# The second MLP product of the first phase in three bf16 terms, with new orders on four engines

## What is computed

```python
x = x + tanh(g_xattn[0]) * L0_xattn(layernorm(x), ctx, ctx, ...)
def L0_xattn(q, k, v, ...):
    log_ratio = log(prob(q)) - log(prob(k))            # prob: tanh, scaled and normalised
    sid = einsum('bnd,bmd->bnm', prob(q) - prob(k), log_ratio)
    attn = softmax(-sid / sqrt(D))
    f_diff = (v - attn @ v) @ W_diff.T + b_diff + q
    h = layernorm(f_diff, ln_g, ln_b)
    mlp = gelu(h @ W1.T + b1) @ W2.T + b2              # W1: 1024 x 256, W2: 256 x 1024
    return layernorm(mlp + f_diff, ln_g, ln_b)
```

## Time and profile before

| | us |
|---|---|
| median of three runs | 1754.54 |
| lowest and highest | 1752.0, 1756.51 |
| the profiled execution, its own time | 1753.54 |
| its span, first to last instruction | 1751.8 |

### The profile page before, as it was taken

How to read it: one execution, slowest core, us unless ns; L and a number is a source line. 1 busy time by engine, 2 the same in 40 slices (tenths; PEclk the granted TensorE clock), 3 DMA queues, 4 the chain that set the end, 5 groups by cost and what they waited for, 6 DMA issues and landing times.

```text
span 1751.8 us, 42950 instructions
## 1 busy us (share of the span) xinstructions
PE 1610.3 (92%) x14411; PEld 1255.7 (72%) x14411; DVE 1336.3 (76%) x3213; ACT 1055.9 (60%) x1894; POOL 1033.6 (59%) x1873
## 2 busy tenths in 40 slices
PE   5999999999999993577999999999999999999997
PEld 4888888888888882344677777767777776767666
DVE  5677777777777766768888888888888888887643
ACT  6666666666666553255656666665666666565654
POOL 5566676667666645324656575665656566564536
PEclk9999999999999996688999999999999999999999
DMA  7312211221122002342233232322223232222200
GB/s 210 101 61 74 76 60 60 75 75 60 60 79 71 7 1 71 96 123 79 82 83 88 79 93 75 90 85 82 81 83 90 72 90 85 83 84 84 66 15 20
DMA packets 215099, 133.59 MB, mean 76 GB/s; under 512 B 45936, under 2 KB 214256, under 8 KB 214768
## 3 DMA queue, kind: packets, MB, share of 16 engines
q1 hardware_dynamic: 215024, 132.61, 25.9%
HBM read 101.07 MB, written 25.17 MB: 72 GB/s over the span
## 4 chain that ended last, share of the span: by engine, by line
PE 34%; DVE 8%; ACT 6%; issue 5%; POOL 5%; SPq 1%; DVEq 0%; DMA 0%; ACTq 0%; POOLq 0%
PE b_bank L1639 17%; PE b_bank L1718 5%; PE b_scoreT L1696 4%; PE b_scoreT L1700 3%; PE b_score L1679 2%; ACT L31 2%; DVE b_v L1522 2%; DVE b_nm L1459 2%; ACT b_Y L1337 2%; ACT b_E L1277 1%; PE b_bank L1647 1%; POOL b_YT L1204 1%; DVE b_hn L1440 1%; PE b_bank L1733 1%; POOL b_rs L1214 1%
## 5 line engine op out<-in xcount | busy, mean ns | idle before, releaser
L1459 DVE TENSOR_REDUCE b_nm<-b_score 128x4 bf16<-128x1024 f32 x256 | 314.5, 1228 | 115.2 <-PE b_score L1679 107.7
L1277 ACT ACTIVATE b_E<-b_scoreT 128x1024 f32<-128x1024 f32 x256 | 262.0, 1023 | 196.9 <-PE b_scoreT L1700 196.0
L1159 POOL TENSOR_TENSOR b_pool_fence<-b_pool_fence 128x1 f32<-128x1 f32 x288 | 67.6, 235 | 299.3 <-ACT b_Y L1337 258.5
L761 PE MATMUL bank<-W2T,G 128*128 128x256 f32 x1024 | 231.2, 379 | 0.0
L761 PEld LDWEIGHTS bank<-W2T,G 128*128 128x128 f32 x1024 | 192.1, 190 | 24.8
L31 ACT ACT_TABLE_LOAD x156 | 200.1, 1283 | 9.9 <-PEq L876 6.6
L1337 ACT ACTIVATE b_Y<-b_bank,b1f 128x256 f32<-128x256 f32 x256 | 107.3, 470 | 159.1 <-PE b_bank L1639 158.7
L1639 PE MATMUL b_bank<-b_hT,f 128*128 128x256 bf16 x1536 | 188.7, 273 | 11.6 <-ACT b_Y L1337 11.3
L1639 PE MATMUL b_bank<-f,b_YT 128*128 128x256 bf16 x1536 | 183.5, 273 | 2.9 <-POOL b_YT L1204 1.9
L328 POOL TENSOR_TENSOR pool_fence<-pool_fence 128x1 f32<-128x1 f32 x256 | 48.3, 201 | 233.5 <-DVE mv L538 145.9
L728 PE MATMUL bank<-hT,W1T 128*128 128x256 bf16 x1536 | 178.3, 273 | 6.6 <-ACT G L498 2.5
(11 more groups left out here) (211 smaller groups left out, 3538.1 us busy)
## 6 DMA issues: line engine op xcount, KB each, us to landing
b_Q<-q_dram SPq DMA_DIRECT2D x256, 64.0 KB, 2.5
b_K<-k_dram SPq DMA_DIRECT2D x256, 64.0 KB, 2.5
xin<-in_x SPq DMA_DIRECT2D x32, 256.0 KB, 4.3
ctxn<-in_ctx SPq DMA_DIRECT2D x32, 256.0 KB, 2.7
mask_in<-in_mask SPq DMA_DIRECT2D x32, 256.0 KB, 3.0
X<-in_x SPq DMA_DIRECT2D x32, 256.0 KB, 4.2
ctxt<-in_ctxT SPq DMA_DIRECT2D x32, 256.0 KB, 4.4
b_ctxt<-in_ctxT SPq DMA_DIRECT2D x32, 256.0 KB, 2.7
```

Source lines behind the costliest of these rows:

```text
L761: last = nc.tensor.matmul(out_ps[:, t], G[w.parity][:, h, t * P:(t + 1) * P], W2T[:, h], start=h == 0, stop=h == HC - 1)
L1277: nc.scalar.activation(E[:, pair:pair + 2], scoreT_ps[:, :, :, :], ACT.Exp).then_inc(sig["E"], 1)
L1459: nc.vector.tensor_reduce(pair, score_ps[:, :, :, :], AX.X, ALU.max, negate=True).then_inc(sig["nm"], 1)
```

## The change

1. `W2T` becomes bf16 with two parts, made once: ACT writes the high part in turn 4 and DVE the low part. The raw weights land in `G`.
2. `G` is one f32 tile instead of two. A new tile `GT` holds gelu's high and low part in bf16. For each quarter j of the hidden width ACT computes `G`, waits for itself, and copies it to the high part (`gelu_high(j)`, L553). The low part, `G` minus high part, is made by DVE for j = 0 and by POOL for j = 1, 2, 3 (`gelu_low(j)`, L768 and L440).
3. `output(t)` is now 24 bf16 matmuls; it waits for the four low parts.
4. On all four engines the steps are issued in another order. On PE `output(0)` moves behind the product with the context; on ACT the gelus come ahead of the tanh; on DVE `probabilities` comes last instead of ahead of `x1`.

```diff
-        W2T = sb("W2T", [P, HC, D], F32, late)
+        W2T = sb("W2T", [P, 2, HC, D], BF16, late)
-        G = two("G", [P, HC, S], F32)
+        G = sb("G", [P, HC, S], F32)
+        GT = sb("GT", [P, 2, HC, S], BF16)
...
+                def gelu_low(j):
+                    pool.wait_ge(sig["Ghi"], done(m, per=HC // 2, part=j + 1))
+                    nc.gpsimd.tensor_tensor(GT[:, 1, 2 * j:2 * j + 2], G[:, 2 * j:2 * j + 2], GT[:, 0, 2 * j:2 * j + 2],
+                                            ALU.subtract).then_inc(sig[f"Glo{j}"], 1)
...
+                def gelu_high(j):
+                    act.wait_ge(sig["G"], done(m, per=HC // 2, part=j + 1))
...
+                    nc.scalar.activation(GT[:, 0, 2 * j:2 * j + 2], G[:, 2 * j:2 * j + 2], ACT.Copy).then_inc(sig["Ghi"], 1)
...
-                    for h in range(HC):
-                        if t == 0 and h % 2 == 0:
-                            pe.wait_ge(sig["G"], done(w, per=HC // 2, part=h // 2 + 1))
-                        last = nc.tensor.matmul(out_ps[:, t], G[w.parity][:, h, t * P:(t + 1) * P], W2T[:, h],
-                                                start=h == 0, stop=h == HC - 1)
+                        for j in range(HC // 2):
+                            pe.wait_ge(sig[f"Glo{j}"], done(w))
+                    last = product(out_ps[:, t], lambda s, k: GT[:, s, k, t * P:(t + 1) * P], lambda s, k: W2T[:, s, k],
+                                   range(HC))
```

More of the change, by code:

```diff
@@ L457, in iteration, with mlp_high @@
                     last.then_inc(sig["E"], 1)
-                if m:
+                def mlp_high():
                     act.wait_ge(sig["hT_mm"], done(m))
@@ L490, in iteration, with gelu, store_x @@
                     last.then_inc(sig["th"], 1)
[L491 to L501, removed]
+                def gelu(j):
+                    act.wait_ge(sig["mlp_mm"], done(m, per=HC // 2, part=j + 1))
+                    if j == 0 and at_batch(m, 0):
+                        act.wait_ge(sig["W2"], 1)
+                    if (due := done(m, back=1)) is not None:
+                        act.wait_ge(sig[f"Glo{j}"], due)
+                    for i in range(2):
+                        last = nc.scalar.activation(G[:, 2 * j + i], mlp_ps[j % 2][:, i], ACT.Gelu,
+                                                    bias=b1c[:, 2 * j + i:2 * j + i + 1])
+                    last.then_inc(sig["G"], 1)
+                def gelu_high(j):
+                    act.wait_ge(sig["G"], done(m, per=HC // 2, part=j + 1))
+                    if j == 0:
+                        if (due := done(m, back=1)) is not None:
+                            act.wait_ge(sig["out_mm"], due)
+                    nc.scalar.activation(GT[:, 0, 2 * j:2 * j + 2], G[:, 2 * j:2 * j + 2], ACT.Copy).then_inc(sig["Ghi"], 1)
+                def store_x():
                     act.wait_ge(sig["x1"], done(w))
@@ L778, in iteration, with scores @@
                     transposed(lT_ps, lr[u.parity], "lT_mm")
[L779 to L788 removed]
+                def scores():
                     pe.wait_ge(sig["dT"], done(u))
@@ L846, in iteration @@
                     last.then_inc(sig["att_mm"], 1)
-                if m:
+                if at_batch(m, 0):
+                    pe.wait_ge(sig["W1"], 1)
+                if at_iteration(half, parity, NB + 2):
+                    pe.wait_ge(sig["base"], NB)
+                    pe.wait_ge(sig["peak_w"], 1)
+                    nc.tensor.transpose(U_ps[0:1, 0, 0:P], peak_w[:, :], ident[:, :]).then_inc(sig["peak_rows"], 1)
+                if u:
+                    logs_transposed()
+                    difference_transposed()
+                if q:
+                    context_product()
+                if w:
+                    output(0)
+                if u:
+                    scores()
+                if m:
+                    mlp_transposed()
+                if w:
+                    output(1)
+                if m:
+                    hidden(0)
+                if u:
+                    exponentials_transposed()
+                if m:
+                    hidden(1)
                     hidden(2)
                     hidden(3)
+                if u:
+                    attention()
+                if at_iteration(half, parity, NB + 2):
+                    pe.wait_ge(sig["peak_all"], 1)
+                    nc.tensor.matmul(U_ps[:, 1, 0:1], second["ones"][:, :], peak_all[:, :], start=True, stop=True).then_inc(
+                        sig["peaks_w"], 1)
                 if at_batch(q, 1):
```

251 lines of the change are left out of this document (165 added, 86 removed).

## The result

| | us, median | lowest to highest | runs |
|---|---|---|---|
| before | 1754.09 | 1752.0 to 1756.51 | 6 |
| after | 1791.42 | 1782.64 to 1838.02 | 6 |

The ratio is 1.0191, with a 95% interval from 1.0165 to 1.0217: 2% slower, where 2.4% was forecast. The ratio leaves out the two longest executions of after as slow ones, but their mean granted clock (0.966 and 0.965) is no lower than in the others (0.962 to 0.968), and the medians of the table, with all six, give 1.0213. Before repeats within 5 us, after spreads over 55 us. The profiled execution of after took 1827.86 us, near the slow end, so a size read from it is above the median's.

A forecast was written before the change was run, and what follows sets the result against it. PE was taken to bound the kernel before, then a POOL and DVE ring: 17.80 + 1.92 + 1.25 = 20.97 us, 1.51 more a turn. 27 turns and +1 gave 1753.5 + 42 = 1796 us, range 1736 to 1815.

The forecast's parts named there:

- PE's gain: On PE, the second MLP product's halves fall from 3.46 to 2.62 us in bf16; a turn from 19.46 to 17.78.
- The sums of the other engines: Work a turn in the first phase: ACT 12.64 to 15.5 us, DVE 14.69 to 15.4, POOL 13.16 to 16.6.
- x1 held, +1.92 a turn: POOL's gelu_low(1) and gelu_low(2) behind `rso` hold DVE's two `x1`, ending at 2.85 us instead of 0.93; chance 0.64.
- The lesser collisions, +1.25: Other SBUF collisions with DVE lengthen POOL's part of the ring by 0.6 to 1.8 us a turn, taken as 1.25.
- The term beside it: POOL's own work between `mvf` and the next `rso`, kept from the kernel before as 12.27 + 1.17 = 13.44 us.
- the last rival: Worse alignment: small DVE instructions (`neg` of `x`) caught behind POOL's `df`, +1.0 us a turn, 1823 us; chance 0.06.
- the ring: DVE from `x1` to `mvf` (4.17 us), POOL to the next `rso` (13.44), handovers (0.19): 17.80, with collisions 20.97.
- The sum: 27 turns of 1.51 us more, +1 for splitting W2, second phase 0: 1753.5 + 42 = 1796 us.
- x1 first: `x1` starts before POOL can hold it and POOL pays; ring 19.05 us, total 1744 (1733 to 1758); chance 0.18.
- No collisions: DVE's and POOL's instructions fall apart in time; turn 17.8 us, total 1707 us; chance 0.12.

The follow-up runs named there:

- xh_before_parts: The changed kernel with POOL's first_normalised (`rsx`, `xh`) moved ahead of its three gelu_low, directly behind `rso`; 1727.28 us, ratio 0.9853.
- the add run: The changed kernel without DVE's negated means; POOL's normalisation adds the mean where it should subtract it; 1783.47 us (one run).
- f32_new_orders: The changed kernel's new step orders, with the second product back in f32, two `G` buffers and no high and low parts; 1750.59 us, ratio 0.9981.
- pool_memset: The changed kernel with POOL's three subtractions each replaced by a fence and two zero memsets, leaving out low parts 1 to 3; 1738.59 us, ratio 0.9917.
- rs_copy_on_act: The changed kernel with the 128x2 copy of `r1` into `rs1` made by ACT behind its logarithms instead of by DVE; 1801.65 us, ratio 1.0249.
- old_orders_bf16: The changed kernel's bf16 product with its split, in the step orders of the kernel before on all four engines; 2017.78 us, ratio 1.1517.

## Why the forecast came out right, and where its steps were off

1. **PE's gain: right.** A turn without waits was put at 17.78 us. xh_before_parts has turns of 17.97 with PE busy for 17.59. The W2 product takes 2.78 us a half where its row showed 3.62, and the page puts it at 179.7 us in all, where "about 170" was forecast.
2. **The sums of the other engines: right.** ACT 15.5, DVE 15.4 and POOL 16.6 were forecast. The turn of xh_before_parts shows 14.86, 15.21 and 17.15, the last with some 0.6 of `xh` beside `x1` in it. ACT's wait for its own gelu was put at 0.1 us with no row behind it; in after `G` ends at 323.48 and the copy starts at 323.51, 0.03 us later. ACT was not on the way that sets the turn, so this changed nothing.
3. **x1 held, +1.92 a turn: the step holds where it happens.** At 326.66 two `x1` end 2.71 us after `rso`; 2.85 was forecast, and 0.93 without POOL. The add run shows it in every turn, +1.74. In the profiled execution of after it is in few: `x1` averaged 658 ns, not the 1.3 to 1.5 us that were to show it.
4. **The lesser collisions, +1.25: right in the first pattern.** They were looked for on POOL, and in the turns with `x1` held they are there: `f` 939 ns and `xb` 1027 in the add run for about 730 alone. From `mvf` to the next `rso` POOL takes 14.4 us in these turns and 13.16 where nothing holds it, +1.2. The term beside it was a little too long: 13.44 was taken for the 13.16.
5. **What the forecast didn't have: the second pattern.** There the same exclusion is paid by the other engine. POOL takes its undisturbed 13.16 us, and DVE pays: two `o` +1.8, the copy +2.55, `GT` +0.85, by the rows at 431.56 to 440.49. `negx` pays 1.0 in both patterns; this was the last rival, with a chance of 0.06, and f32_new_orders shows it with the new orders alone. The step that fails in this pattern is the path: the ring has `x1` start when `rso` is there, but `rso` is ready 5.1 us earlier, and the turn is closed by `mvf`, POOL's `xh` and DVE's row behind it (4.17 + 4.27 + 13.99 = 22.4 us). The forecast's rows had a one-input instruction held (`b_v`), but not one of 128x2 held for longer than one instruction of POOL.
6. **The sum: good, and in part by luck.** The ring of the first pattern is 5.89 + 14.42 + 0.09 = 20.4 us in the add run, where 6.09 + 14.69 + 0.19 = 20.97 was forecast. The second pattern takes 22.4. The forecast of 1796 us lies between the add run (1783.5, all turns of the first) and the slowest execution (1838). An estimate from the turns fits: 27 turns of 22.4 in place of 20.4 are 54 us more, 1837 after 1783.5. By the same count an execution at the median of after, 1791, would be mostly in the first pattern, but none of that length was profiled, so this isn't shown. Nothing in the forecast said how often the second pattern would come.
7. **The rivals.** "x1 first" would have given 1744. In the second pattern `x1` is indeed free, but only behind two `o` that have paid, and the turn is 22.4 and not 19.05. pool_memset is nearer to it: `x1` is free, and the ring is 4.17 + 14.33 + 0.09 = 18.6 us. "No collisions", put at 1707 (its own terms add up to 1709), was the best that a right order can reach: xh_before_parts with 1727.3 comes near to it. The remaining 20 us were not taken apart.

The page "SBUF — State Buffer" of the Trainium skill, section "Who interferes with whom", lets a Vector instruction and POOL get into each other's way in two cases. In the first the Vector instruction has two SBUF inputs while POOL reads SBUF. `x1`, `o`, `lr` and `GT` agree with it (2.2 to 3 times their length in the held cases above). In the second it is a copy or a `tensor_scalar` with one input that runs in a mode using both of the engine's ports. The copy of 128x2 and `negx` can be of this kind: they take up to 2.73 and 1.27 us beside POOL's two-input instructions, for 0.18 alone. No view of this case shows in which mode they ran. By the page POOL's memsets, which only write, hold up no two-input instruction of DVE; pool_memset agrees, with `o` at 473 ns and `x1` at 482.

## What to carry to other kernels

When work is moved to POOL, ask of each instruction with two SBUF inputs what DVE does in that microsecond; with the same three instructions this kernel was 37 us slower than before in one order and 27 us faster in another. If a DVE instruction is far longer than its shape, moving it may only get its neighbour held, as in rs_copy_on_act: find the POOL instruction that started about 0.1 us ahead and try another order there. Follow both ways through a turn, that of the semaphores and that of each engine's own row, since either can be the longer. And where a kernel's executions differ by 3%, take several profiles before sizing any one collision.

## What the runs showed of the hardware that was not expected

- POOL's two-step instruction on 128x256 f32 takes 553 ns as (add, mult) and 1224 as (subtract, mult) for `xh1`, 627 and 1297 for `xh`, which stands beside DVE's `hn` (in pool_memset it takes 556). Only the operation matters: with the operand of the slow one, the add is as fast as before. The negated means, which look like waste, save 2.7 us of POOL a turn for 0.35 of DVE where nothing holds them.
- A DVE copy of 128x2 that came 0.11 us after the first of four back-to-back instructions of POOL waited for all four, 2.73 us. In other turns it got in after the first (0.61 us at 321.56, when it came 0.15 after the start of `f`). Why it isn't let in between in the one case stays open.
- In old_orders_bf16, after 8.3 us of idle time on PE, the granted clock was 0.50 (the 1.2 GHz level) through the next 5.1 us, and 24 matmuls took twice their time. In after, with pauses of at most 1.34 us in the turn shown, the clock stayed at 1.00.
